# ViT tower kernel on one core: the expert biases as one product per block, the token weights turned and written as one tile

## The reference, cut to what matters

```python
logits = xf @ Wr.T + br
probs = jax.nn.softmax(logits, axis=-1)
top2_prob, top2_idx = jax.lax.top_k(probs, 2)
comb = jnp.zeros((n, e), x.dtype).at[jnp.arange(n)[:, None], top2_idx].add(top2_prob)
h = jax.nn.gelu(jnp.einsum('nd,edh->enh', xf, W1) + b1[:, None, :], approximate=False)
o = jnp.einsum('enh,ehd->end', h, W2) + b2[:, None, :]
y = jnp.einsum('ne,end->nd', comb, o)
```

## Time and profile before

| | us |
|---|---|
| median of 3 executions (250.4 to 253.96) | 251.33 |
| the profiled execution, its own time | 250.8 |
| its span, first to last instruction | 248.8 |
| PE busy | 229.9 |
| DVE busy | 191.6 |
| ACT busy | 161.7 |
| POOL busy | 62.9 |

### The profile page before, as it was taken

One profiled execution on the slowest core, in us unless ns is written; L12 is line 12 of the kernel. 1 busy time (PEld: TensorE's weight loads), 2 busy tenths in 40 slices (PEclk: granted clock), 3 DMA queues, 4 the chain that ended last, 5 costly groups with the idle time before them and its releaser, 6 DMA issues.

```text
span 248.8 us, 6293 instructions
## 1 busy us (share of the span) xinstructions
PE 229.9 (92%) x2316; PEld 194.3 (78%) x2316; DVE 191.6 (77%) x483; ACT 161.7 (65%) x504; POOL 62.9 (25%) x96
## 2 busy tenths in 40 slices
PE   1999999999998889989999999899899999999993
PEld 1845675899776766658788999789799999999972
DVE  1676788774768899998186838678999989989991
ACT  2551569752199899993025977422699798898880
POOL 8824132096005465469212300000000000000000
PEclk9999999999999999999999999999999999999999
DMA  6980000000004427064000000079888410001011
GB/s 141 334 228 0 4 0 1 3 3 0 3 0 82 91 68 105 4 211 131 3 7 3 0 3 0 11 100 139 143 214 280 156 35 16 17 4 32 0 42 34
DMA packets 15625, 16.46 MB, mean 66 GB/s; under 512 B 1747, under 2 KB 14367, under 8 KB 15468
## 3 DMA queue, kind: packets, MB, share of 16 engines
q1 hardware_dynamic: 14424, 15.59, 26.2%
q0 software_dynamic: 544, 0.35, 0.6%
q10 hardware_dynamic: 628, 0.14, 0.3%
HBM read 13.91 MB, written 2.16 MB: 65 GB/s over the span
## 4 chain that ended last, share of the span: by engine, by line
PE 55%; DVE 14%; issue 11%; POOL 11%; DMA 4%; ACT 2%; SPq 1%; DVEq 0%; POOLq 0%
PE banks L1332 51%; POOL region_e L472 5%; DMA region_a<-in_x 4%; DVE KT L1290 2%; POOL w_lo L529 2%; DVE top L1030 1%; DVE stb L994 1%; POOL region_d L479 1%; PE banks L1535 1%; POOL rstd L414 1%; DVE stb L913 1%; PE banks L1676 1%; DVE stats L892 1%; PE banks L1842 1%; PE banks L1483 1%
## 5 line engine op out<-in xcount | busy, mean ns | idle before, releaser
L762 ACT ACTIVATE w_sb<-banks,vecs 128x416 f32<-128x416 f32 x60 | 36.3, 606 | 11.0 <-PE banks L1332 9.2
L680 ACT ACTIVATE region_e<-banks,ntop 128x64 f32<-128x64 f32 x128 | 38.2, 344 | 5.1 <-DVE ntop L1037 4.8
L770 ACT ACTIVATE y_hi<-w_sb 128x416 fp32r<-128x416 f32 x60 | 32.7, 547 | 8.1 <-DVE w_sb L1264 8.1
L1273 DVE TENSOR_TENSOR y_lo<-w_sb,y_hi 128x416 fp32r<-128x416 f32 x60 | 34.9, 584 | 1.0 <-ACT y_hi L770 1.0
L680 ACT ACTIVATION_READ_ACCUMULATOR region_e<-banks,ntop 128x1 f32 x128 | 29.6, 237 | 0.0
L1332 PE MATMUL banks<-x_hi,w_hi 128*128 128x416 f32 x80 | 29.1, 364 | 0.0
L1332 PE MATMUL banks<-x_lo,w_hi 128*128 128x416 f32 x80 | 28.2, 352 | 0.0
L1332 PE MATMUL banks<-x_hi,w_lo 128*128 128x416 f32 x80 | 28.0, 350 | 0.0
L1264 DVE TENSOR_TENSOR w_sb<-w_sb,region_c 128x416 f32<-128x416 f32 x40 | 23.4, 586 | 2.1 <-ACT w_sb L762 1.4
L1332 PE MATMUL banks<-y_hi,w_hi 128*128 128x416 f32 x60 | 22.2, 369 | 1.4 <-DVE KT L1290 1.0
L1332 PE MATMUL banks<-y_hi,w_lo 128*128 128x416 f32 x60 | 21.1, 351 | 0.0
(11 more groups left out here) (243 smaller groups left out, 504.7 us busy)
## 6 DMA issues: line engine op xcount, KB each, us to landing
region_c<-out SPq DMA_DIRECT2D x4, 832.0 KB, 14.6
xnT<-out SPq DMA_DIRECT2D x5, 208.0 KB, 14.1
QT<-out SPq DMA_DIRECT2D x5, 208.0 KB, 13.6
region_a<-in_x SPq DMA_DIRECT2D x2, 512.0 KB, 5.0
region_a<-in_x SPq DMA_DIRECT2D x1, 1024.0 KB, 9.7
out<-h SPq DMA_DIRECT2D x2, 512.0 KB, 6.2
h<-out SPq DMA_DIRECT2D x4, 256.0 KB, 5.0
w_sb<-in_L_ffn_W SPq DMA_DIRECT2D x1, 1024.0 KB, 5.8
```

Of the source, the lines that this page charges most:

```text
L680: last = a.activation(dst[:, h // 2, h % 2], src[:, h // 2, h % 2], ACT.Exp, scale=SCALE, bias=ntop[:, o + h:o + h + 1], accum_out=esum[:, ...
L762: a.activation(lifted(u), bank[h_bank(i)][:, 0:FB], ACT.Gelu, bias=vecs[:, b:b + 1])\
L770: a.activation(h_hi(u), lifted(u), ACT.Copy).then_inc(S["hi_ok"], 1)
L1273: v.tensor_tensor(h_lo(u), lifted(u), h_hi(u).bitcast(F32), ALU.subtract).then_inc(S["lo_ok"], 1)
```

## The change

The biases leave the direct way. Each token tile of `combP` now gets, beside each other, the weights of the eight experts three times: rounded, rounded again, and the remainder that the rounding left (POOL, after `comb_ok`, told by `cs_ok`). `b2r` holds rows that fit them, 32 in all of which 24 are not zero. After the turn the rows are lined up by ACT in `crow`, 32 partitions x 2080 tokens (five copies), and `down_sum` ends each block with one product of `b2r` and `crow`. `base` is gone on PE and DVE, and the ring of banks holds the direct experts alone; `down_sum` collects in banks 6 and 7 and `turn_back` uses 4 and 5.

The token weights for `weigh` no longer come from `combT`. DVE writes them in expert order (`cw`, 16 token tiles x 8 experts as 128 columns), PE turns this tile at once in the middle of the third `down` group, ACT copies it, and SP writes it by one transfer of 128 rows of 512 bytes. In memory an expert's row is then 2048 tokens long (2080 before); the 32 class tokens are a second small tile and go by a transfer of their own, issued after block 1, and three transfers of 32 columns (128 bytes per row) follow block 4, whose own rows end at 384 columns. `d_wb2` counts these as well.

The scalings of DVE around the first steps are reordered. The constant tile `kc` grows by one column; in the built program the tiles behind it (`region_c`, `region_d`, `QT`, `KT`, `xnT`) begin 32 bytes later, and some tiles of the early stages share their place with late ones.

The core of the diff (renamed semaphores and moved allocations are left out):

```diff
         def out_expert(e, g):
 
-            n = 5 * e + g
-            return n if n < AHEAD else n + 7
+            return 5 * e + g
...
             sp_.wait_ge(S["d_h0q"], 64)
-            sp_.wait_ge(S["cT_ok"], 2)
-            for c in range(2):
-                sp_.dma_start(scratch(c * P, [[ALL, E - DIRECT], [4 * P, 4], [1, P]]),
-                              combT[32 * c + DIRECT:32 * c + E, 0:4 * P].rearrange("e (g m) -> e g m", g=4))\
-                    .then_inc(S["d_cs"], 16)
-            sp_.dma_start(scratch(TOK, [[ALL, E - DIRECT], [1, IMG]]), combT[DIRECT:E, 4 * P:4 * P + IMG])\
-                .then_inc(S["d_cs"], 16)
-            sp_.wait_ge(S["d_cs"], 16 * 5)
+            sp_.wait_ge(S["cw_ok"], 1)
+            sp_.dma_start(scratch(0, [[P, P], [1, P]]), cwT).then_inc(S["d_cs"], 16)
+            sp_.wait_ge(S["d_cs"], 16)
...
+                if blk == 1:
+                    sp_.wait_ge(S["cw_ok"], 2)
+                    sp_.dma_start(scratch(E * TOK, [[IMG, E], [1, IMG]]), cwC).then_inc(S["d_cs"], 16)
+            sp_.wait_ge(S["d_cs"], 32)
+            sp_.dma_start(four[:, :, TOK:ALL], scratch(E * TOK + DIRECT * IMG, [[0, P], [IMG, 4], [1, IMG]]))\
+                .then_inc(S["d_wb2"], 16)
+            for e in range(6, 8):
+                sp_.dma_start(weights(e)[:, TOK:ALL], scratch(E * TOK + e * IMG, [[0, P], [1, IMG]]))\
+                    .then_inc(S["d_wb2"], 16)
...
+            pool.wait_ge(S["comb_ok"], 1)
+            cc = cw[0:IMG, PAIRS * E:NT * E]
+            g.tensor_copy(comb[0:IMG, PAIRS, E:3 * E].rearrange("p (r e) -> p r e", r=2).bitcast(F32R),
+                          cc.unsqueeze(1).to_broadcast([IMG, 2, E]))
+            link(g.tensor_copy(comb[:, 0:PAIRS, E:3 * E].rearrange("p t (r e) -> p t r e", r=2).bitcast(F32R),
+                               cwm.unsqueeze(2).to_broadcast([P, PAIRS, 2, E])))
+            g.tensor_tensor(comb[0:IMG, PAIRS, 3 * E:4 * E].bitcast(F32R), cc, comb[0:IMG, PAIRS, E:2 * E], ALU.subtract)
+            g.tensor_tensor(comb[:, 0:PAIRS, 3 * E:4 * E].bitcast(F32R), cwm, comb[:, 0:PAIRS, E:2 * E], ALU.subtract)\
+                .then_inc(S["cs_ok"], 1)
...
+            act.wait_ge(S["cw_ps"], 1)
+            a.activation(cwT, bank[7][:, 0:P], ACT.Copy).then_inc(S["cw_ok"], 1)
+            a.activation(cwC, bank[7][0:E, P:P + IMG], ACT.Copy).then_inc(S["cw_ok"], 1)
...
             for u in range(G_RING - 1):
                 lift(u)
+            for c in range(4):
+                a.activation(crow[0:4 * E, 0:TOK].rearrange("p (g c m) -> p g c m", g=4, c=4)[:, :, c, :],
+                             combT[32 * c:32 * c + 4 * E, 0:4 * P].rearrange("p (g m) -> p g m", g=4), ACT.Copy)
+            a.activation(crow[0:4 * E, TOK:ALL], combT[0:4 * E, 4 * P:4 * P + IMG], ACT.Copy).then_inc(S["crow_ok"], 1)
...
-                    if (e, g) == (0, AHEAD):
-                        for c in range(5):
-                            base(c)
...
-                    if (e, g) == (1, 2):
+                    if (e, g) == (1, 1):
                         weigh(0)
                         weigh(1)
-                    if (e, g) == (1, 3):
+                    if (e, g) == (1, 2):
+                        rest(0)
                         weigh(2)
-                        rest(0)
+                        rest(1)
...
+            def turn_weights_of_tokens():
+                pe.wait_ge(S["comb_ok"], 1)
+                t_.transpose(bank[7][:, 0:P], cw[:, 0:P], ident)
+                t_.transpose(bank[7][0:E, P:P + IMG], cw[0:IMG, PAIRS * E:NT * E], ident[0:IMG, 0:IMG])\
+                    .then_inc(S["cw_ps"], 1)
...
-            down(0, 2)
-            pe.wait_ge(S["comb_ok"], 1)
-            pe.wait_ge(S["acc_ok"], 2)
+            down(0, 2, turn_weights_of_tokens)
+            pe.wait_ge(S["gelu_ok"], 20)
+            pe.wait_ge(S["cs_ok"], 1)
+            pe.wait_ge(S["cw_ok"], 2)
             for g in range(4):
...
-            for g in range(4):
-                for c in range(4):
-                    last = base(c, g)
...
-                    pe.wait_ge(S["acc_ok"], 15)
+                    pe.wait_ge(S["acc_ok"], out_expert(1, 1) + 1)
...
+                if e == E - 1:
+                    pe.wait_ge(S["crow_ok"], 1)
+                    last = mm(o, b2r[0:4 * E, :], crow[0:4 * E, blk * FB:(blk + 1) * FB], False, True)
```

More of the change, by code:

```diff
@@ L137, in vit_kernel @@
         RKB = relk_bd[:, :].rearrange("p (r s) -> p r s", s=2)
-        wnT = sb("wnT", 512)
-        q0w = wnT[:, 0:56]
-        q0r = wnT[:, 64:96]
-        WnT = wnT[:, :].rearrange("p (w r o) -> p w r o", w=2, r=2)
-        w3 = sb("w3", C)
-        wqkvo = sb("wqkvo", 4 * C)
-        wq, wk, wv, wo = (wqkvo[:, i * C:(i + 1) * C] for i in range(4))
         rows = sb("rows", P)
@@ L205, in vit_kernel @@
         RV = RVBD[:, :].rearrange("p (q s d) -> p q s d", q=QC, s=2)
+        stb = early_sb("stb", 1024)
+        tmpx = early_sb("tmpx", 8 * QC)
+        wnT = early_sb("wnT", 512)
+        w3 = early_sb("w3", C)
+        wqkvo = early_sb("wqkvo", 4 * C)
+        ST = [stb[:, 0:512], stb[:, 512:1024]]
+        q0w = wnT[:, 0:56]
+        q0r = wnT[:, 64:96]
+        WnT = wnT[:, :].rearrange("p (w r o) -> p w r o", w=2, r=2)
+        wq, wk, wv, wo = (wqkvo[:, i * C:(i + 1) * C] for i in range(4))
         early.close()
@@ L221, in vit_kernel @@
         accT = region_d[:, 0:ALL]
+        crow = ctx.enter_context(nc.sbuf_tensor("crow", [P, ALL], F32R))
+        b2t = y_hi[0:4 * E, 0:C]
+        b2n = posb[0:4 * E, :]
         def weights(e):
@@ L365, in _ @@
             for blk in range(1, 5):
-                b = slice(blk * FB, (blk + 1) * FB)
-                sp_.dma_start(region_c[:, :].rearrange("p (e t) -> p e t", e=4)[:, :, b],
-                              scratch(blk * FB, [[0, P], [ALL, 4], [1, FB]])).then_inc(S[f"d_wb{min(blk, 2)}"], 16)
+                b = slice(blk * FB, min((blk + 1) * FB, TOK))
+                n = b.stop - b.start
+                sp_.dma_start(four[:, :, b], scratch(DIRECT * TOK + blk * FB, [[0, P], [TOK, 4], [1, n]]))\
+                    .then_inc(S[f"d_wb{min(blk, 2)}"], 16)
@@ L402, in _ @@
             g.dma_start(brb[:, :], br.unsqueeze(0).to_broadcast([P, E])).then_inc(S["d_small"], 16)
-            for c in range(4):
-                g.dma_start(b2s[32 * c:32 * c + E, :], fb2).then_inc(S["d_small"], 16)
+            for c in range(1, 4):
+                g.dma_start(b2s[E * c:E * c + E, :], fb2).then_inc(S["d_small"], 16)
             link(g.memset(mhalf[:, :], -0.5))
+            g.memset(b2s[0:E, :], 0.0)
             pool.wait_ge(S["ve_c"], 1)
@@ L545, in _ @@
             deviation2(4)
+            link(g.tensor_copy(b2t, b2s[0:4 * E, :]))
+            link(g.tensor_scalar(b2n, b2t.bitcast(F32), kc[0:4 * E, K_NM:K_NM + 1], None, ALU.mult))
+            g.tensor_tensor(b2r[0:4 * E, :], b2s[0:4 * E, :], b2n, ALU.add).then_inc(S["b2_ok"], 1)
+            pool.wait_ge(S["comb_ok"], 1)
[7 more added lines that the diff above has]
+                .then_inc(S["cs_ok"], 1)
         @block.scalar
@@ L1761, in _, with down @@
             up(0, 4)
-            def down(e, g):
+            def down(e, g, between=None):
                 tiles = GROUPS[g]
@@ L1776, in down @@
                                   w2_sb[:, e, s, :], s == 0, s == 1)
+                    if between and i == 1:
+                        between()
                 last.then_inc(S["y2_ps"], 1)
-            def base(c, g, m=P):
-                r = slice(32 * c, 32 * c + E)
-                o = bank[out_bank(out_base(c))][0:m, g * P:(g + 1) * P] if g < 4 else bank[out_bank(out_base(4))][0:m, 0:C]
-                return mm(o, combT[r, g * P:g * P + m], b2s[r, :])
+            def turn_weights_of_tokens():
[3 more added lines that the diff above has]
+                    .then_inc(S["cw_ps"], 1)
             pe.wait_ge(S["d_ffn"], 16)
@@ L1829, in down_sum @@
                     mm(o, w2_lo[:, w], h_hi(u), False, False)
-                    last = mm(o, w2_hi[:, w], h_lo(u), False, e == E - 1 and s == 1)
+                    last = mm(o, w2_hi[:, w], h_lo(u), False, False)
+                if e == E - 1:
+                    pe.wait_ge(S["crow_ok"], 1)
+                    last = mm(o, b2r[0:4 * E, :], crow[0:4 * E, blk * FB:(blk + 1) * FB], False, True)
                 last.then_inc(S["y3_ps"], 1)
```

124 lines of the change are left out of this document (53 added, 71 removed).

## The result

The forecast was 250.0 us in a range of 248.3 to 253.6. The changed kernel has a median of **257.1 us** over 21 executions (252.81 to 286.89), the kernel before 251.7 over 21 in the same comparison: **slower**, and outside the range. The profiled execution took 257.1 us, with a span of 255.3.

A forecast was written before the change was run, and what follows sets the result against it. PE's unbroken products were the bound, to be started earlier. From 250.8, 1.8 us gained at block 2 less 0.76 for four bias products gave 249.8; set between profiled and median times: 250.0, range 248.3 to 253.6.

The forecast's parts named there:

- The step that failed: Token-weight transfers: the 18 start at 158.8, 2.9 us earlier, so their end moves equally, from 199.5 to 196.6.
- a forecast gain of 1.8 us at this place: PE's second half of the collecting step at block 2: begins at 200.2 instead of 201.98, with a landing at 198.0.
- The rule of the step behind it: Block 2: PE cannot begin its second half before the last token-weight landing plus 2.2 us.
- after it PE without gaps: Expected profile sign: behind DVE's wait of 1 to 2 us at block 2, PE runs unbroken with five short products more.
- The three transfers: New 32-column transfers ending the stream: nothing by bytes, 7.5 us by row count; landing taken as 198.0 instead of 196.6.
- rival (b): First scaling of block 2: 128-byte rows cost by count, 9.8 ns each, giving 255.9 us at full price; chance 23%.
- the rule on 32 bytes in front of a piece: Stream destinations beginning 32 bytes later: one beat more in 52 to 56, 0.7 us, making the time 250.5.
- The bias product: One per block on PE, five in all: 0.19 us each, 0.95 together; upper bound 0.35 each.
- The shift: First collecting products on PE start earlier, through removed waits and bias work: 2.9 us, bounds 2.5 to 3.1.
- The 72 products of the direct experts: PE's last run before the collecting products: begins 2.0 us earlier, at 162.7, and takes 8.52 us.
- DVE's run behind them: DVE busy without a gap from expert 1's second group, its last remainder letting PE start the second half at about 175.8.
- POOL's gather: Ahead of PE's turn of `combP`: 1.07 to 1.24 us, done by 156.9, covered by 0.7 us.

The follow-up runs named there:

- E9: Changed kernel with the token weights' memory rows 2080 tokens apart instead of 2048, its three 32-column transfers kept; 250.5 us, ratio 0.9969 to the kernel before.
- E3: Changed kernel with 21 more products on PE just ahead of its wait at block 2; 255.4 us, ratio 1.0113 to the kernel before.
- E7: Kernel before, with SP issuing block 4's three transfers only after nine PE steps, so block 2's scaling waits; 261.8 us, a single execution.
- E5: Changed kernel with only the three 32-column transfers on their own semaphore, awaited by block 4; 255.4 us, ratio 1.0113 to the kernel before.
- E13: Changed kernel with the constant tile at its old size, so destinations begin where they did before, rows 2048 apart; 256.7 us, ratio 1.0095.
- E15: Kernel before with memory rows 4096 tokens apart and destination tiles 32 bytes later; 251.8 us, ratio 0.9984.
- E4: Changed kernel with separate semaphores for blocks 2, 3 and 4 and the bias product over 128 partitions instead of 32; 249.3 us, ratio 0.987.
- E12: Changed kernel with two edits alone, memory rows 2080 tokens apart and the bias product over 128 partitions; 248.7 us, ratio 0.990 to the kernel before.
- E11: Kernel before with the token weights' memory rows 4096 tokens apart instead of 2080; 253.1 us, ratio 1.0023.
- E16: Changed kernel with 18 whole-row transfers, memory rows 4096 tokens apart, only experts 2 to 7 written, from the start of memory; 254.4 us, ratio 1.0007.
- E10: Changed kernel with 18 whole-row transfers, one semaphore for blocks 2 to 4, memory rows 4096 tokens apart; 252.4 us, ratio 0.9991 to the kernel before.
- E2: Changed kernel with the class tokens' write issued ahead of the stream instead of in its middle; 256.9 us, ratio 1.0151 to the kernel before.

## Why the prediction was wrong

**The step that failed** is "nothing that they wait for is on the engines, so I move the whole stream: its end from 199.5 to 196.6". The stream was not the same one: the change had set its memory rows 2048 tokens apart where they had been 2080. The description of the change tells of this, and the prediction has no term for it: it priced it at nothing, without a reason. E9 shows the price, a stream of 42.9 us against 36.0, by that edit alone; the forecast had 39.2 (198.0 less 158.8). It turned a forecast gain of 1.8 us at this place into a loss of 1.6 (203.57 against 201.98). The rule of the step behind it, PE not before the landing plus 2.2, held: 201.3 + 2.2 = 203.5.

**A term that was missing: the granted clock.** The prediction had "after it PE without gaps" and counted a gap at its own length. A gap of 3.88 us took 2.9 more from the products behind it (E3; E7 shows it without the change). Without that the result would have been 254.2, just outside the range.

**The three transfers**, on which rival (b) rested and for which I took 1.4 us, cost 0.6 at most (E5), and E9 has them all and is a little faster than before. Rival (b) named the right place and the right side, and its sign, a wait above 3 us, came (5.02), but for a cause that was not there: that its full price, 255.9, lies near 257.1 is luck. For the rule on 32 bytes in front of a piece, which I had set at 0.7 us, E13 to E15 show no loss, and an effect of that size would be lost in the scatter of single profiles. My estimate also stretched it: the Trainium skill (DMA: Bandwidth & Descriptors, section How a descriptor splits into AXI transactions) tells it of bytes that are fetched, and here the destinations moved.

**The bias product** was mis-sized: 0.19, with 0.35 as the upper bound, and measured 0.58. The bounds came from products of one shape in a row; what costs here is the change of shape between neighbours (E4).

**The shift** was 3.5 us, taken as 2.9 with 3.1 as its bound. The 72 products of the direct experts began at 162.30, where I had 162.7, and DVE's run behind them came as laid out. POOL's gather took 1.5 us where I had 1.07 to 1.24, and ended 0.3 us before PE's turn, where I had 0.7. This gain is real: 0.9 us came through with the distance mended (E9's median against 251.4 before), 3.0 with the bias in its neighbours' shape as well (E12's against 251.7).

Put together at PE's second half at block 2: 1.6 lost there, 2.9 by the clock, and four bias products behind it, three at 0.58 and the last, which nothing follows at once, at 0.37, are 6.6. The spans differ by 255.3 − 248.8 = 6.5, the own times by 257.1 − 250.8 = 6.3.

**What stays open:** why the distance slows the reads at all, and why more in the changed kernel's forms. There the stream is 4.6 to 8.4 us longer at 2048 tokens than at 2080, and 2.7 to 4.6 longer at 4096; in the form of the kernel before it is at most 1.5 longer at 4096, and 2048 was not tried. The 32 bytes and the place of the first row were tried and don't tell. The way in which the rows are written, which differs between the two forms, was not tried, and with the distance the place of every later row moves too, which these runs can't tell apart.

## What to carry to other kernels

When a change moves a transfer earlier, look at what it does to the transfer's addresses first: here a new distance of rows cost more than the earlier start brought, and the diff showed it in one number. A stall of TensorE is to be priced with its echo: here 2.9 us for 3.9 of standing still, so one semaphore for all later blocks turns a late byte that nobody needs yet into a loss nearly twice its length. The small product between large ones was cheaper in their shape, padded with zeros.

## What was not expected of the hardware

- Reading rows of 1664 bytes to 128 partitions from memory rows 8192 bytes apart took 41.3 to 44.4 us for the whole stream in seven profiles; 8320 bytes apart 36.0 to 36.7 in four profiles of the changed kernel's forms. In the form of the kernel before, 16384 bytes took 38.1 to 39.2, 8320 bytes 37.7 and 38.7.
- A product over 32 partitions between products over 128 took 0.58 us of PE's time, and 0.19 when padded to 128.
- Gaps of PE of 0.65, 1.25 and 2.11 us (E11, E16, E5) left the granted clock full; behind gaps of 2.23, 2.79, 2.85, 3.88 and 7.71 (E13, E10, E2, after, E7) it went to 0.50 for some 3 to 10 us. The Trainium skill (TensorE: Matmul & The Clock Gate, section What's actually happening) ties the clock to how busy PE has been of late; E3 agrees: with products in the gap the clock stayed at 1.00.
